# Stacking the heads' outputs into three chunks of 128 rows before the output projection of a grouped attention

## The reference, cut to what matters

```
q = (latents @ Wq.T).reshape(b, q_len, H, HD)            # H 16, HD 96
k, v = hidden @ Wk.T, hidden @ Wv.T                      # KV 4 heads of 96, over context and latents
scores = einsum('bkgqd,bksd->bkgqs', q, k) * scale
attn = softmax(scores)
out = einsum('bkgqs,bksd->bkgqd', attn, v)
return out @ Wo.T                                        # contraction over 16 * 96
```

## Time and profile before

| what | us |
|---|---|
| median of 3 runs | 1997.21 |
| the profiled execution | 1992.77 |
| its span, first to last instruction | 1991.0 |
| third stage, by its windows | about 981 (1010 to 1991) |
| PE busy in the span | 1905.9 (96%) |
| DVE, ACT, POOL busy in the span | 1073.7, 910.2, 618.4 |
| mean granted TensorE clock | 0.965 |

### The profile page before, as it was taken

The page is one execution under the profiler, slowest core; times in us unless marked ns, Lnnn a source line. Parts: engine busy times, 40 slices in busy tenths (PEclk is TensorE's granted clock), DMA queues, the critical chain, the costliest instruction groups (busy, mean ns, idle before and its releaser), DMA issues. The chain is left out here.

```text
span 1991.0 us, 23522 instructions
## 1 busy us (share of the span) xinstructions
PE 1905.9 (96%) x8690; PEld 1356.3 (68%) x8690; DVE 1073.7 (54%) x2058; ACT 910.2 (46%) x1726; POOL 618.4 (31%) x504
## 2 busy tenths in 40 slices
PE   7999997999999999999889999999999999999997
PEld 6999894444565465555677777767777777767763
DVE  3554435676666665666445555555555455554414
ACT  3333331444344344344146666635665455655650
POOL 0000000000000000000047766746676566765660
PEclk9999995999999999999989999999999999999996
DMA  5977953000111020030293444313444143343111
GB/s 196 289 242 242 291 188 97 0 1 17 53 36 56 11 74 27 17 88 22 88 216 88 106 116 105 87 36 89 116 106 105 40 108 92 87 106 83 33 32 43
DMA packets 169561, 190.69 MB, mean 96 GB/s; under 512 B 86329, under 2 KB 144833, under 8 KB 166374
## 3 DMA queue, kind: packets, MB, share of 16 engines
q1 hardware_dynamic: 167652, 188.92, 35.1%
q10 hardware_dynamic: 1794, 0.27, 0.1%
HBM read 117.11 MB, written 71.99 MB: 95 GB/s over the span
## 5 line engine op out<-in xcount | busy, mean ns | idle before, releaser
L1392 POOL TENSOR_TENSOR pl<-pf,ph 128x512 fp32r<-128x512 f32 (+1 forms) x480 | 610.7, 1289 | 309.4 <-ACT pf L1570 307.6
L1567 ACT ACTIVATE ph<-ps 128x512 fp32r<-128x512 f32 (+1 forms) x480 | 288.6, 601 | 394.4 <-PE ps L1467 393.4
L1626 DVE TENSOR_REDUCE pm<-ps 128x1 f32<-128x464 f32 x480 | 307.5, 642 | 163.8 <-PE ps L1410 153.5
L1138 DVE TENSOR_REDUCE pm<-ps 128x1 f32<-128x400 f32 (+3 forms) x544 | 285.4, 572 | 90.9 <-PE ps L985 86.9
L1045 ACT ACTIVATE pr<-ps 128x512 f32<-128x512 f32 (+1 forms) x416 | 219.6, 601 | 196.0 <-PE ps L917 195.2
L1570 ACT ACTIVATE pf<-ps 128x512 f32<-128x512 f32 (+1 forms) x480 | 289.2, 602 | 0.3 <-POOL pl L1392 0.3
L1381 POOL MEMSET vh<- 128x30 f32 x1 | 0.2, 153 | 699.9 <-POOLq L682 699.9
L930 PE MATMUL ps<-pr,cv 128*64 128x512 f32 (+1 forms) x832 | 210.6, 622 | 0.0
L1485 PE MATMUL ps<-ph,vh 128*97 128x512 f32 (+1 forms) x480 | 194.9, 406 | 0.0
L1488 PE MATMUL ps<-pl,vh 128*97 128x512 f32 (+1 forms) x480 | 190.1, 396 | 0.5 <-POOL pl L1392 0.3
L1486 PE MATMUL ps<-ph,vl 128*97 128x512 f32 (+1 forms) x480 | 189.9, 396 | 0.0
(11 more groups left out here) (255 smaller groups left out, 3178.7 us busy)
## 6 DMA issues: line engine op xcount, KB each, us to landing
woT<-wo_turned SPq DMA_DIRECT2D x16, 1536.0 KB, 9.0
v_scr<-vst SPq DMA_DIRECT2D x16, 1152.0 KB
cnat<-in_ctx_dram SPq DMA_DIRECT2D x16, 768.0 KB
q_scr<-qst SPq DMA_DIRECT2D x48, 256.0 KB, 2.5
vh<-v_scr SPq DMA_DIRECT2D x15, 672.0 KB
vl<-v_scr SPq DMA_DIRECT2D x15, 672.0 KB
home<-k_scr SPq DMA_DIRECT2D x14, 696.4 KB, 8.3
k_scr<-home SPq DMA_DIRECT2D x24, 384.0 KB, 7.8
```

The costliest lines, as they stand in the source:

```text
L1138: dve.reduce_max(pm[:, j, ch:ch + 1], src[:, 0:(cuts if s < S else next_cuts)[ch][1]], AX)\
L1392: pool.tensor_tensor(pl[0:m, n % 2, cols], pf[0:m, half, :], ph[0:m, n % 2, cols].bitcast(F32), ALU.subtract).then_inc(plo, 1)
L1567: act.activation(ph[0:keys[kt], n % 2, cols], src, ACT.Exp, scale=S1).then_inc(phi, 1)
L1626: ins = dve.reduce_max(pm[:, j, ch:ch + 1], at[:, 0:cuts[ch][1]], AX)
```

## The change

For groups 0 to 14 the projection is done from another layout; group 15's stays as it was, with its own copy of Wo's slice (`woL`, loaded once near the start of the stage). For the others:

- the row of sums is sent at the end of its group, right behind ACT's copies of `o`. DVE inverts it in the 8 x 128 layout ("invert"), ACT sends it to DRAM (`send_parts`, after the exponentials of tile 2), ACT reads it back onto 96 partitions (`spread_parts`, after tile 3), and DVE multiplies `o` by it ("normal");
- ACT sends the normalised `o` to DRAM (`send_o`, after tile 6) and reads it back as three chunks of 128 rows (`stack_o`, after tile 7); ACT rounds it (`stacked_hi`, after tile 9) and DVE subtracts ("low");
- four "stacked" items, one for each row tile and half of the 512 columns, each of nine products with 128 rows and 256 columns, take the place of the eight "out" items. DVE adds each of them to x without a factor. The "sum" item with its two products is gone;
- "invert", "normal" and "low" are places in the list, but take no bank. The maxima begin at once and end one step later (kt = 12) than before; the "stacked" items stand in steps 10 and 11;
- `load_wo` waits for the last "stacked" item instead of the last "out".

```
-            order, maxima = (maxima[:12] if s < S - 1 else [None] * 12 * (s < S)) + [("sum", s - 1, 0)], maxima[12:]
-            for i in range(TT * G):
-                order += maxima[:2] + [("out", s - 1, i)] + later[i]
-                maxima = maxima[2:]
-            return order + maxima + ([("dl", e, 0)] if e >= 0 else [])
+            later = [("turn", e, 0), ("turn", e, 1), ("h", e, 0), ("h", e, 1), ("z", e, 0), ("h8", e, 0), ("dl", e, 0)] \
+                if e >= 0 else [None] * 7
+            most = maxima or [None] * NI
+            own = [(kind, s - 1, 0) for kind in ("invert", "normal", "low")]
+            order = most[:6] + own[:1] + most[6:14] + later[:2] + own[1:2] + most[14:19] + later[2:3] + most[19:23] + later[3:4] + most[23:26] + later[4:6] + \
+                most[26:28] + later[6:] + [None, None] + own[2:] + [None]
+            for i in range(NO):
+                order += [("stacked", s - 1, i), most[28 + i]]
+            return order
...
-                    sp.wait_ge(ring_mm, ring["out", s - 1, TT * G - 1] + 1)
+                    sp.wait_ge(ring_mm, ring["stacked", s - 1, NO - 1] + 1)
...
+                elif kind == "stacked":
+                    if i == 0:
+                        pe.wait_ge(wo_in, 32 * (a + 1))
+                        pe.wait_ge(osh_done, a + 1)
+                        pe.wait_ge(osl_done, a + 1)
+                    t, m0 = i // (D // OW), i % (D // OW) * OW
+                    n_mm = 0
+                    for left, part in ((osh, 0), (osh, 1), (osl, 0)):
+                        for c in range(OC):
+                            mm = pe.matmul(at[:, 0:OW], left[:, c, t * P:(t + 1) * P], woT[:, part, c, m0:m0 + OW],
+                                           start=(n_mm == 0), stop=(n_mm == 3 * OC - 1))
+                            n_mm += 1
...
-                act.copy(oh[:, :], o[0:HD1, :]).then_inc(oh_done, 1)
+            def send_parts(s):
+                act.wait_ge(rec_done, s + 1)
+                act.dma_start(sum_scr[0].rearrange("(j m) -> j m", j=QT), recs[:, :]).then_inc(rec_out, 16)
+            def spread_parts(s):
+                act.wait_ge(rec_out, 16 * (s + 1))
+                act.dma_start(orec[:, :], sum_scr.to_broadcast([HD1, GC])).then_inc(rec_in, 16)
+            def send_o(s):
+                act.wait_ge(on_done, s + 1)
+                act.dma_start(o_scr.rearrange("g d t -> d g t"), o[0:HD1, :].rearrange("d (g t) -> d g t", g=G))\
+                    .then_inc(o_out, 16)
+            def stack_o(s):
+                act.wait_ge(o_out, 16 * (s + 1))
+                act.dma_start(os[:, :, :], o_scr.rearrange("g d t -> (g d) t").rearrange("(c p) t -> p c t", p=P))\
+                    .then_inc(os_in, 16)
+            def stacked_hi(s):
+                act.wait_ge(os_in, 16 * (s + 1))
+                act.copy(osh[:, :, :], os[:, :, :]).then_inc(osh_done, 1)
...
+                    if s:
+                        step = {2: send_parts, 3: spread_parts, 6: send_o, 7: stack_o, 9: stacked_hi}.get(kt)
+                        if step:
+                            step(s - 1)
...
+                send_sums(s)
...
+            def invert(s):
+                dve.wait_ge(sum_in, 16 * (s + 1))
+                dve.reciprocal(recs[:, :], sums[:, :]).then_inc(rec_done, 1)
+            def normal_o(s):
+                dve.wait_ge(rec_in, 16 * (s + 1))
+                dve.tensor_tensor(o[0:HD1, :], o[0:HD1, :], orec[:, :], ALU.mult).then_inc(on_done, 1)
+            def stacked_lo(s):
+                dve.wait_ge(osh_done, s + 1)
+                dve.tensor_tensor(osl[:, :, :], os[:, :, :], osh[:, :, :].bitcast(F32), ALU.subtract).then_inc(osl_done, 1)
```

More of the change, by code:

```diff
@@ L1203, in grouped_attention @@
     FIRST = 4
+    OC = G * HD1 // P
+    OW = D // 2
+    NO = TT * D // OW
+    OWN = ("invert", "normal", "low")
     with ExitStack() as ctx:
@@ L1281, in beside @@
                 return [None] * 12 + maxima
+            if s == S:
+                return [("sum", s - 1, 0)] + [("out", s - 1, i) for i in range(TT * G)]
             e = (s - 1) // KV1 - 1 if s % KV1 == 1 else -1
[L1283 to L1289 removed]
+            later = [("turn", e, 0), ("turn", e, 1), ("h", e, 0), ("h", e, 1), ("z", e, 0), ("h8", e, 0), ("dl", e, 0)] \
[7 more added lines that the diff above has]
+            return order
         def last_batch():
@@ L1301, in grouped_attention @@
             for item in beside(s) + (last_batch() if s == S else []):
-                if item:
+                if item and item[0] not in OWN:
                     ring[item] = len(ring)
@@ L1357, in _ @@
             load_q(2, 0)
+            for part in range(2):
+                sp.dma_start(woL[:, part, :, :].bitcast(F32), wo_scr[KV1 - 1, part].rearrange("h d m -> d h m"))\
+                    .then_inc(wol_in, 16)
             for s in range(S):
-                if 0 < s:
+                if 0 < s < S - 1:
                     load_wo(s)
@@ L1587, in _ @@
                 if s:
-                    act.wait_ge(ring_mm, ring["out", s - 1, TT * G - 1] + 1)
+                    act.wait_ge(o_out, 16 * s)
                 for half in range(2):
                     act.copy(o[0:HD1 + 1, half * BANK:(half + 1) * BANK], bank(OB + half)[0:HD1 + 1, :]).then_inc(o_done, 1)
-            send_sums(S - 1)
+                send_sums(s)
+            act.copy(oh[:, :], o[0:HD1, :]).then_inc(oh_done, 1)
             act.wait_ge(to_exp, 1)
@@ L1616, in ring_item @@
                     dve.wait_ge(mxr_done, a - 1)
-                if kind == "sum" and a:
-                    dve.wait_ge(*read("out", a - 1, TT * G - 1))
                 if kind == "out":
                     dve.wait_ge(*(read("out", a, i - TT) if i >= TT else read("sum", a, 0)))
-                    if i == 0:
+                if kind == "stacked":
+                    if a % KV1:
+                        dve.wait_ge(*read("stacked", a - 1, i))
+                    elif i == 0:
                         dve.wait_ge(x_in, 16 * (a // KV1 + 1))
@@ L1662, in fill @@
                         item = next(items, None)
-                        if item:
+                        if item and item[0] in OWN:
+                            {"invert": invert, "normal": normal_o, "low": stacked_lo}[item[0]](s - 1)
+                        elif item:
                             ring_item(*item)
```

49 lines of the change are left out of this document (33 added, 16 removed).

## The result

The changed kernel took 1985.6 us (median of 6 runs, 1982.09 to 1990.34) against 1999.45 for the kernel before on the same chip (6 runs, 1996.5 to 2001.38): a ratio of 0.9936, interval 0.9922 to 0.995. It is faster, by 13.9 us, where the prediction had 25 (1972 from 1997.21): a little over half. Its profiled execution took 1983.97 us with a span of 1982.2, where the sum said 1968.

The account below looks back on a forecast made before the run. PE's own work was taken to bound the kernel; 25.5 us less on PE minus 1.5 for ACT gave 24, called 25: profiled 1992.8 to 1968, median 1972. Own range 1963 to 1981; 8 in 10, 1960 to 1988.

Parts of the forecast that it names:

- PE's part: PE in groups 0 to 14: cheaper products gain 1.3 us a group, dropping the "sum" item 0.40; 25.5 us less in all.
- The rival in which weight loads bound them: PE's 256-column stacked products: loads don't overlap, 6.8 us a group, 13 us slower, 2010 us; chance 0.03.
- Layer-norm groups: Third-stage groups with a layer norm: about 2.4 us each lost to idle time, part at lower clock; stall expected to stay.
- the rival in which it vanishes: Layer-norm groups lose their stall as the rhythm shifts: up to 12 us more gain, 1960 us; chance 0.05.
- ACT in group 15: Last group, no maxima to hide ACT's delays at send, normal and low: 1.5 us lost once.
- DVE's steps: DVE's added and removed operations: less work in sum, holding up nobody while the DMAs have landed; cost 0.
- POOL and the shared port: DVE's normal and low beside POOL: cost 0 taken; rival has POOL late every group, 16 us lost, 1988 us, chance 0.08.
- SP and the loads of `wo`: SP's queue: load_wo about 9 us later, as two issues, and two loads of woL; cost 0.
- The DMA chain: Transfers from ACT's copy of o to stacked rounding: small ones take 3 to 4 us, waits stay within slack; cost 0.
- The rival of the round trips: Small transfers into full queues take 8 us, DVE and ACT block, PE loses 4 us a group; 2032 at worst, chance 0.10.
- the port: DVE and POOL taking turns at SBUF: POOL late at normal and low each group, 16 us lost, 1988 us; chance 0.08.

## Why the prediction was right in direction and short in size

**PE's part: right.** 1.7 us a group was the sum (1.3 for the products, 0.4 for the `sum` item); where nothing waits, it is 1.8, and the pace of the 256-column products is 0.119 us for 0.118. The rival in which weight loads bound them is false: their bound of 6.8 us a group would show as 55.9 us, not 53.2.

**Layer-norm groups: better than forecast, in part by luck.** They gained 6.8 us where PE's part three times is 5.4. But the stall grew (3.1 to 3.4 us of idle time in each, 2.4 before), so this is not the rival in which it vanishes: PE's part less the longer stall would be about 3 us. The rest goes with the granted clock, 1.00 after and 0.98 and 0.95 in groups 5 and 9 before. Why the clock held, no run here separates; over the runs above it differs between kernels with the same work in these groups. Without it, the gain would have been smaller still.

**ACT in group 15: too dear.** 1.5 us were set; the group gained 1.1 where 1.7 - 1.5 = 0.2 was left, so 0.6 is nearer.

**DVE's steps: nearly right.** The reciprocal of 128 columns takes 0.94 us (I took 1.0) and the additions 0.43 (0.4). `low` takes 1.5 us, where I had 1.0, and `normal` 2.0 when it meets POOL and 1.2 when not, where I had 1.2 to 1.8. With the loads held these sizes cost PE nothing in an ordinary group.

**POOL and the shared port: right.** 0 was taken, 16 us the rival. The row behind POOL grew by 8.4 us, but with held loads and both operations in full it is back at 2.9, and the groups take 53.2. Taking `normal` away alone gave 0.1 to 0.3 us a group, on one run, about what two profiles of the changed kernel differ by.

**SP and the loads of `wo`: right.** Nothing waited for them.

**The DMA chain: this step failed.** "I take 3 to 4 us, nearer to the idle row, as its packets come from another queue than SP's ... Cost 0." The sums took 6.6 to 8.6 us in the ten groups that lost time, and from `send_parts` to `spread_parts` ACT needed 3.4 to 4.9. The bound of 1.9 to 9.8 us had held the true value; I chose in it by an argument on queues that no row carried, and gave the cost of the other end to a rival. Nor was I right that the trace doesn't tell: its packet records for the kernel before have the sums' packets 5.3 to 6.5 us after the issue in groups 1 to 13. That price, set against consumers that want the sums 6 us and the parts 10 us into the group, gives waits on DVE and ACT, and they give PE's loss: 1.67 us in each of ten groups, 16.7 us. Hold the loads or move the places, and it is gone; two kernels show it for each.

**The rival of the round trips: right in mechanism, wrong in size.** It had an 8-us transfer, `invert` at 9, DVE blocked from 6 on and the ring stopped: all of that is in the rows above. But it priced the loss at 4 us a group and so ended at 2032. 1.67 is what it was, and in ten groups, not fifteen: in groups 5, 9 and 13 `invert` stands behind the layer norm and doesn't wait, and in groups 14 and 15 less or nothing is loading. I had added up the delays of the waiting engines (2 us by the ring, 1 us for each of two tiles), while most of each is absorbed: after the wait DVE works off five maxima in 2.75 us and has caught up. By its own break-even, 1.7 us a group, it was a near thing: the loss took the gain of the ordinary groups almost entirely (3.3 of 20.0 us left, 1.8 of them in group 14), and the rest of the gain is that of the layer-norm groups, some of it the clock's, and of the last one.

That the time, 1985.6 us, lies inside the wide range of 1960 to 1988 is no merit of the sum: the upper end was there for the port, and it was the transfers that took the time. The forecast's own range, 1963 to 1981, missed it.

The idle rows also understate the loss. Group 8 takes 54.81 us, 1.6 more than 53.2, with 0.98 us of idle time:

```profile
1466.56:1521.37 54.81, 53.83 (x250) 41.49 (x249) 27.11 (x41) 32.99 (x65) 39.04 (x31) 1.00 0.47 118
```

The rest stands in PE's busy column: the same 250 products have 53.83 us there, and 53.20 in this group with held loads. The length of the group against an undisturbed one is the honest measure.

## What to carry to other kernels

The price of a small transfer is set by the traffic around it: here the sums went behind the key and query loads issued a few microseconds before, on another queue. Look up what the loading engine issues in that time, and place the consumer behind the end of that burst (here, the 14th place instead of the 6th), or hold the burst until the chain is through: either turned a gain of 0.6% into one of 1.4 to 1.6%. And if a bound is wide and its upper end costs more than the change brings, design for the upper end: moving the consumer cost nothing here.

## What the hardware did that I had not expected

- 4 KB from ACT's queue took 1.8 us from issue to use with idle DMA engines, 6.0 in a group with fewer loads, and 6.6 to 8.6 behind loads of some 250 GB/s. Most of it passed before the first of its packets ran.
- A DVE operation with two SBUF operands on 2 columns took 146 ns alone and up to 1195 ns beside a POOL subtraction, ending with it; two such in a row each paid it (1.23 and 1.21 us).
- Identical code ahead of the third stage put its first product anywhere within 4.9 us (1010.17 to 1015.06) over eight runs (seven kernels and the changed one again). A change of a few microseconds should be read from its own stage.
